# A graph-attention layer: ten sets of adjacency rows loaded with the projection, the first unit made by blocks, s and t read by ScalarE and compared by GpSimd, later q stores held back

## Chip, core and metric

The kernel runs on one core of a Trainium2 chip. The time is device microseconds of one launch. Its engines are TensorE (PE; PEld is its weight load), VectorE (DVE), ScalarE (ACT), GpSimd (POOL) and SyncE (SP), which only issues transfers. GpSimd issues transfers too.

## What is computed

The inputs are `x` (8192 x 256, float32), an adjacency matrix `adj` (8192 x 8192, int32) of zeros and ones, and the parameters of one attention layer.

```python
h = jnp.maximum(_layernorm(x, axis=-1), 0.0)
Wh = h @ W_w + W_b
e = leaky_relu((Wh @ a1)[:, None] + (Wh @ a2)[None, :], negative_slope=0.2)
attention = jnp.where(adj > 0, e, NEG)
attention = jax.nn.softmax(attention, axis=1)
out = x + attention @ Wh
```

## The kernel before

The work has two stages.

**The projection** goes over the 64 blocks of 128 rows of x, in 32 pairs p. VectorE makes the layer norm's statistics and factors (`norms`; nine groups, `GROUPS`, of 4, 4 and then 8 blocks; the last step of a group, L464, releases the blocks of it). GpSimd (`normalise`, L279; ScalarE for the first four blocks) applies the factors. TensorE transposes a pair (L747), ScalarE copies it out with the relu (`copy_hT`, L329), and TensorE multiplies it by the weights (`project`, L756). Two extra columns of the product are s and t, the two halves of e. VectorE reads them out of PSUM (`read_s_t`, L479), takes the smaller t of the pair (`greater_t`, L484; t is carried with its sign turned), ScalarE makes exponentials of it (`column_exps`, L334) and scales the product into the high half of a split float16 pair (`x_high`, L339), and VectorE makes the low half (`x_low`, L489), which frees the PSUM slot; there are six slots. In the course of it GpSimd issues the loads of the first eight sets of adjacency rows (a set is 128 rows by a quarter of the columns, 256 KB as read, issued as 4 quadrants by `load_quadrant`, L285), and VectorE transposes them (`transpose`, L586) beside the last eight pairs.

Between the stages, VectorE reduces t over all columns and makes q, a factor of each row. SyncE stores the first piece of q to memory, loads it back broadcast over the partitions (`load_q`, L229) and stores the rest. GpSimd's further loads wait for that load.

**The attention** has 8 rows s of 1024 output rows each, and in each row 32 units k of 2 blocks of 128 columns. A unit is made in a ring of four: ScalarE makes the products (`product`, L362, two halves of 1024), VectorE the weights (`weights`, L656), ScalarE their high half (`high`, L377), VectorE the low half (`low`, L663); then TensorE does 48 matmuls on it (`unit`, L789). Eight units are a chunk g; while a chunk is made, VectorE transposes the eight sets of the next (`turn`). TensorE sums all of a row into the eight PSUM banks. At the end of a row VectorE divides and adds x (`finish`, L671 and L674), and the next row's first matmul of a bank (`start`, L793) waits for that. After the projection VectorE also makes a mean (L643 to L647) which TensorE's first `start` needs.

The order on each engine is the order in which the code is written: no scheduler moves anything. Every engine works through its own list and waits on semaphores.

## Time and profile before

| | |
|---|---|
| median of 3 runs | 1485.84 us (1485.68 to 1487.18) |
| the profiled execution | 1486.66 us |
| its span, first to last instruction | 1484.9 us |
| TensorE busy | 98% |
| VectorE busy | 96% |
| ScalarE busy | 73% |
| GpSimd busy | 41% |
| mean granted TensorE clock | 0.992 of full speed |

A matmul counts as busy while it is modelled to run, so 98% says that TensorE nearly always has work, not that it runs at its peak. The busy shares are means over stages with different limits: the projection lasts to 91 us of the span, the first attention row to 283 us, and the seven other rows fill the rest.

### The profile page before, as it was taken

Reading aid. Unit: us, or ns where it says so; the run is one execution under the profiler, and the core shown is the slowest. Engines: PE = TensorE matmul, PEld = TensorE weight load, DVE = VectorE, ACT = ScalarE, POOL = GpSimd, SP = SyncE. Lnnn points to the kernel's source line nnn. Section 1 sums busy time; section 2 is a strip of 40 time slices with the busy share of each in tenths; the row PEclk is TensorE's granted clock in tenths of the full one; section 3 lists DMA queues with packets and bytes.
Section 4 is the critical chain, followed back from the end, with each engine's and each line's share of the span. In section 5 each row is a group of like instructions: output and inputs, shape, how many; then the busy total and the mean of one; then the engine's idle time right before and its main releaser. Section 6 shows DMA issues by size and latency. Waiting matters only on the chain.

```text
span 1484.9 us, 29899 instructions
## 1 busy us (share of the span) xinstructions
PE 1450.0 (98%) x12746; PEld 1261.6 (85%) x12746; DVE 1421.7 (96%) x1263; ACT 1086.0 (73%) x1006; POOL 605.4 (41%) x1106
## 2 busy tenths in 40 slices
PE   6969999999999999999999999999999999999998
PEld 5848888888888888888888888888888888888887
DVE  8989999999999999999999999999999999999993
ACT  4768888687777777687776877777776877777771
POOL 4748444354443444354442544344432544433000
PEclk9989999999999999999999999999999999999999
DMA  9729997798778977799777977699677887788000
GB/s 215 86 26 131 98 73 55 108 82 61 51 65 102 84 51 51 85 97 69 52 64 95 86 53 51 60 117 75 48 61 102 77 61 51 51 102 70 2 1 29
DMA packets 179559, 107.53 MB, mean 72 GB/s; under 512 B 20065, under 2 KB 176353, under 8 KB 179425
## 3 DMA queue, kind: packets, MB, share of 16 engines
q0 software_dynamic: 155904, 75.56, 68.1%
q1 hardware_dynamic: 23520, 30.05, 6.9%
q8 instruction: 100, 1.64, 0.4%
q14 instruction: 35, 0.28, 0.1%
HBM read 298.45 MB, written 8.42 MB: 207 GB/s over the span
## 4 chain that ended last, share of the span: by engine, by line
PE 81%; DVE 15%; DMA 1%; issue 1%; POOL 0%; SPq 0%; ACT 0%; DVEq 0%
PE acc L789 80%; DVE work L663 4%; DVE work L656 4%; DVE xr L437 1%; DVE adj_cols L586 1%; DVE X L489 1%; DMA adj_rows<-in_adj 1%; PE acc L756 1%; PE acc L793 0%; DVE xr L448 0%; DVE xr L484 0%; DMA work<-q_rows 0%; POOL adj_rows L285 0%; DVE xr L473 0%; DVE xr L469 0%
## 5 line engine op out<-in xcount | busy, mean ns | idle before, releaser
L789 PE MATMUL acc<-X,work 128*128 128x257 f16 x12288 | 1367.6, 273 | 7.1 <-DVE work L663 7.1
L789 PEld LDWEIGHTS acc<-X,work 128*128 128x128 f16 x12288 | 1189.8, 97 | 178.8 <-DVE work L663 7.6
L285 POOL DMA_DIRECT2D adj_rows<-in_adj x1024 | 551.3, 548 | 721.4 <-DVE adj_cols L586 684.8
L377 ACT ACTIVATE work<-work 128x2048 f16<-128x2048 f32 x256 | 488.0, 1909 | 292.2 <-PE acc L789 269.8
L663 DVE SCALAR_TENSOR_TENSOR work<-work 128x2048 f16<-128x2048 f32 x256 | 585.3, 2286 | 26.6 <-ACT work L377 26.5
L656 DVE SCALAR_TENSOR_TENSOR work<-work,sigma,adj_cols 128x2048 f32<-128x2048 f32 x256 | 595.1, 2325 | 5.7 <-ACT work L362 2.2
L362 ACT ACTIVATE work<-q_odd,r_j 128x1024 f32<-128x1024 f32 x256 | 278.5, 1135 | 23.9 <-DVE work L663 23.9
L362 ACT ACTIVATE work<-work,r_j 128x1024 f32<-128x1024 f32 x256 | 278.5, 1136 | 23.4 <-DVE work L663 18.2
L586 DVE STREAM_TRANSPOSE adj_cols<-adj_rows 128x512 int32<-128x512 int32 x256 | 177.1, 701 | 1.4 <-DMA adj_rows<-in_adj 1.4
L756 PE MATMUL acc<-q_odd,adj_cols 128*128 128x258 f32 x256 | 64.4, 396 | 0.7 <-ACT adj_cols L329 0.6
L756 PEld LDWEIGHTS acc<-q_odd,adj_cols 128*128 128x128 f32 x256 | 48.0, 197 | 8.7 <-ACT adj_cols L329 2.1
L279 POOL TENSOR_SCALAR work<-work,xr 128x256 f32<-128x256 f32 x60 | 33.6, 564 | 32.4 <-DVE xr L464 31.3
L747 PE MATMUL acc<-q_odd,work 128*128 128x128 f32 x128 | 21.5, 289 | 13.2 <-ACT work L320 9.9
L747 PEld LDWEIGHTS acc<-q_odd,work 128*128 128x128 f32 x128 | 16.2, 146 | 18.4 <-issue 11.9
L437 DVE BATCH_NORM_STATS2 xr<-work 128x6 f32<-128x256 f32 x64 | 25.4, 417 | 3.9 <-DMA work<-in_x 3.7
L489 DVE SCALAR_TENSOR_TENSOR X<-acc,c_j,X 128x256 f16<-128x256 f32 x64 | 28.6, 473 | 0.0
L334 ACT ACTIVATE c_j<-xr 128x2 f32<-128x2 f32 x32 | 9.5, 296 | 25.8 <-DVE xr L484 25.3
L674 DVE SCALAR_TENSOR_TENSOR xr<-acc,rden,xr 128x256 f32<-128x256 f32 x64 | 26.6, 478 | 0.6
L339 ACT ACTIVATE X<-acc,c_j 128x256 f16<-128x256 f32 x64 | 26.8, 476 | 0.0
L329 ACT ACTIVATE adj_cols<-acc 128x256 f32<-128x256 f32 x64 | 23.4, 369 | 0.1
L295 POOL DMA_DIRECT2D xr<-in_L_gnn_W_b x16 | 21.4, 1622 | 1.0 <-issue 1.0
L793 PE MATMUL acc<-mean_wh,tiny 128*128 128x257 f16 x64 | 17.2, 291 | 2.8 <-DVE mean_wh L647 1.6
(76 smaller groups left out, 84.4 us busy)
## 6 DMA issues: line engine op xcount, KB each, us to landing
adj_rows<-in_adj POOLq DMA_DIRECT2D x1024, 64.0 KB, 4.2
xr<-in_x SPq DMA_DIRECT2D x16, 512.0 KB, 4.6
xr<-in_L_gnn_W_b POOLq DMA_DIRECT2D x16, 512.0 KB, 17.0
out<-xr SPq DMA_DIRECT2D x16, 512.0 KB, 5.4
work<-in_x SPq DMA_DIRECT2D x28, 256.0 KB, 15.1
work<-q_rows SPq DMA_DIRECT2D x4, 512.0 KB, 5.4
q_odd<-q_rows SPq DMA_DIRECT2D x4, 512.0 KB, 5.7
work<-in_x SPq DMA_DIRECT2D x8, 128.0 KB, 3.3
```

The costliest lines, as they stand in the source:

```text
L279: nc.gpsimd.tensor_scalar(x_in[:, b, :], x_in[:, b, :], rstd[:, b:b + 1], shift[:, b:b + 1], ALU.mult, ALU.add).then_inc(s_hp, 1)
L285: pool.dma_start(rows8[QP * q:QP * (q + 1), n % R8], adj_v[s, m, k, q]).then_inc(s_rows[n % R8], 16)
L362: ins = nc.scalar.mul(Wt[:, i % RING, e, :], q_bc[s % 2], r_j[:, 2 * k + e:2 * k + e + 1])
L377: nc.scalar.mul(Et[:, at:at + 2, 0, :], Wt[:, i % RING], SCALE).then_inc(s_H, 1)
L437: nc.vector.bn_stats(st[:, b % XG + n, :], x_in[:, b + n, :]).then_inc(s_bn, 1)
L489: nc.vector.scalar_tensor_tensor(out=X16[:, b, 1, 0:F], in0=ps_wh[:, b % WH, 0:F], scalar=c_j[:, b:b + 1], in1=X16[:, b, 0, 0:F], op0=ALU. ...
L586: nc.vector.transpose(rows.rearrange("p w (q r) -> p q w r", q=SQ), rows8[:, n % R8].bitcast(I32).rearrange("p q (w c) -> p q w c", w=CW)) ...
L656: nc.vector.scalar_tensor_tensor(out=slot, in0=slot, scalar=sigma[:, k:k + 1], in1=edges, op0=ALU.max, op1=ALU.min).then_inc(s_M, 1)
L663: nc.vector.scalar_tensor_tensor(out=Et[:, at:at + 2, 1, :], in0=Wt[:, i % RING], scalar=SCALE, in1=Et[:, at:at + 2, 0, :], op0=ALU.mult, ...
L747: ins = nc.tensor.transpose(ps_hT[p % 2][:, (2 * c + e) * P:(2 * c + e + 1) * P], x_in[:, b, c * P:(c + 1) * P], ident)
L756: ins = nc.tensor.matmul(ps_wh[:, b % WH, 0:F2], hT[:, p % 2, c, e * P:(e + 1) * P], Wx[:, c, :], start=(c == 0), stop=(c == KF - 1))
L789: return nc.tensor.matmul(acc[:, m, 0:F1], Et[:, 2 * (k % RING) + e, 1 if n == 2 else 0, m * P:(m + 1) * P], X16[:, 2 * k + e, 1 if n == 1 ...
```

## The change

It has five parts.

1. `read_s_t` moves from VectorE to ScalarE, and `greater_t` from VectorE to GpSimd. On ScalarE, `copy_hT` of the pair after next now stands ahead of `column_exps`. GpSimd's `greater_t(p)` stands ahead of the normalisation of block 2p + 8.
2. Ten sets of adjacency rows instead of eight are loaded in the course of the projection: GpSimd issues a quadrant behind three of four blocks, instead of two of three. VectorE transposes the two added sets between the denominator columns and the mean.
3. The first unit of the first row is made in two blocks, with semaphores of their own, so that each step and TensorE's first 24 matmuls wait for one block only.
4. On ScalarE the product of unit 2 now stands behind both high halves of unit 0.
5. SyncE stores the rest of q only when the loaded q has landed.

```diff
+    AHEAD = 10
@@ SyncE
             load_q(0)
+            sp.wait_ge(s_q, 16)
             store_q(0, NZ // 2, NZ, s_qst)
@@ GpSimd
+            def greater_t(p):
+                pool.wait_ge(s_st, p + 1)
+                if p == 0:
+                    pool.wait_ge(s_lnx, 1)
+                nc.gpsimd.tensor_scalar(t_top[:, p:p + 1], s_t[:, 2 * p, 1:2], s_t[:, 2 * p + 1, 1:2], sc[:, 12:13],
+                                        ALU.min, ALU.add).then_inc(s_tt, 1)
             for b in range(4, NB):
+                if b >= 8 and b % 2 == 0:
+                    greater_t(b // 2 - 4)
                 normalise(b)
-                turn, at = divmod(b - 4, 3)
-                if at < 2 and 2 * turn + at < NQ * SETS:
-                    load_quadrant(*divmod(2 * turn + at, NQ))
+                turn, at = divmod(b - 4, 4)
+                if at < 3 and 3 * turn + at < NQ * AHEAD:
+                    load_quadrant(*divmod(3 * turn + at, NQ))
+            for p in range(PAIRS - 4, PAIRS):
+                greater_t(p)
             pool.wait_ge(s_q, 16)
-            for n in range(SETS, NSET * NS):
+            for n in range(AHEAD, NSET * NS):
@@ ScalarE
             for p in range(PAIRS + 1):
+                if p >= 1:
+                    read_s_t(p - 1)
                 if p >= 2:
                     x_high(2 * p - 4)
                     x_high(2 * p - 3)
+                if p + 1 < PAIRS:
+                    copy_hT(p + 1)
                 if p >= 1:
                     column_exps(p - 1)
-                if p + 1 < PAIRS:
-                    copy_hT(p + 1)
...
-            product(0, 0)
+            act.wait_ge(s_q, 16)
+            nc.scalar.mul(Wt[:, 0, 0, :], q_bc[0], r_j[:, 0:1]).then_inc(s_W0, 1)
+            nc.scalar.mul(Wt[:, 0, 1, :], q_bc[0], r_j[:, 1:2]).then_inc(s_W, 1)
+            act.wait_ge(s_M0, 1)
+            nc.scalar.mul(Et[:, 0, 0, :], Wt[:, 0, 0, :], SCALE).then_inc(s_H0, 1)
+            act.wait_ge(s_M, 1)
+            nc.scalar.mul(Et[:, 1, 0, :], Wt[:, 0, 1, :], SCALE).then_inc(s_H, 1)
             product(0, 1)
-            high(0, 0)
             product(0, 2)
             high(0, 1)
@@ VectorE
                 norms(p, 0)
-                if p >= 1:
-                    read_s_t(p - 1)
                 norms(p, 1)
-                if p >= 1:
-                    greater_t(p - 1)
                 norms(p, 2)
...
+            for m in range(AHEAD - SETS):
+                transpose(1, m)
             dve.wait_ge(s_tot, 1)
...
-                if g + 1 < NC * NS:
+                if g + 1 < NC * NS and SETS * g + m >= AHEAD - SETS:
                     transpose(g + 1, m)
...
-            weights(0, 0)
+            first_weights(0, s_W0, s_M0)
+            first_weights(1, s_W, s_M)
+            first_low(0, s_H0, s_E0)
+            first_low(1, s_H, s_E)
@@ TensorE
-            unit(0, 0)
+            pe.wait_ge(s_E0, 1)
+            block_of_unit(0, 0)
+            pe.wait_ge(s_E, 1)
+            block_of_unit(0, 1)
```

GpSimd's list in the middle of the projection. `work<-work,xr` is `normalise` of one block, `DMA` one quadrant of rows. Before:

```order
L279 TENSOR_SCALAR work<-work,xr 128x256 [waits norm_factors_ready] x2
L285 DMA adj_rows<-in_adj 32x4x512
L279 TENSOR_SCALAR work<-work,xr 128x256 [waits norm_factors_ready]
L285 DMA adj_rows<-in_adj 32x4x512
L279 TENSOR_SCALAR work<-work,xr 128x256 [waits norm_factors_ready] x2
```

Now (`xr<-xr,sc 128x1` is `greater_t`):

```order
L293 TENSOR_SCALAR xr<-xr,sc 128x1 [waits s_t_read]
L285 TENSOR_SCALAR work<-work,xr 128x256 [waits norm_factors_ready]
L299 DMA adj_rows<-in_adj 32x4x512
L285 TENSOR_SCALAR work<-work,xr 128x256 [waits norm_factors_ready]
L299 DMA adj_rows<-in_adj 32x4x512
L293 TENSOR_SCALAR xr<-xr,sc 128x1 [waits s_t_read]
L285 TENSOR_SCALAR work<-work,xr 128x256 [waits norm_factors_ready]
L299 DMA adj_rows<-in_adj 32x4x512
L285 TENSOR_SCALAR work<-work,xr 128x256 [waits norm_factors_ready]
```

A comparison now stands ahead of every second block and waits for ScalarE's read, and the quadrants stand closer.

VectorE's list from the end of the mean's preparation to unit 3's weights. `X<-c_j,X` is the last instruction ahead of the mean, the `mean_wh` rows are the mean, `work` rows are weights (with `sigma`) and low halves. Before:

```order
L641 TENSOR_TENSOR X<-c_j,X 128x64 [waits vector_chain]
L643 CAST mean_wh<-sc 1x1 [waits mean_wh_in_psum]
L647 TENSOR_TENSOR mean_wh<-mean_f,xr 1x256
L656 SCALAR_TENSOR_TENSOR work<-work,sigma,adj_cols 128x2048 [waits adj_transposed,products_ready] x2
L663 SCALAR_TENSOR_TENSOR work<-work 128x2x1024 [waits weights_hi_ready]
L586 STREAM_TRANSPOSE adj_cols<-adj_rows 128x4x4x32 [waits adj_loaded8]
L656 SCALAR_TENSOR_TENSOR work<-work,sigma,adj_cols 128x2048 [waits adj_transposed,products_ready]
L663 SCALAR_TENSOR_TENSOR work<-work 128x2x1024 [waits weights_hi_ready]
L586 STREAM_TRANSPOSE adj_cols<-adj_rows 128x4x4x32 [waits adj_loaded9]
L656 SCALAR_TENSOR_TENSOR work<-work,sigma,adj_cols 128x2048 [waits adj_transposed,products_ready]
L663 SCALAR_TENSOR_TENSOR work<-work 128x2x1024 [waits weights_hi_ready]
```

Now:

```order
L655 TENSOR_TENSOR X<-c_j,X 128x64 [waits vector_chain]
L602 STREAM_TRANSPOSE adj_cols<-adj_rows 128x4x4x32 [waits adj_loaded8]
L602 STREAM_TRANSPOSE adj_cols<-adj_rows 128x4x4x32 [waits adj_loaded9]
L659 CAST mean_wh<-sc 1x1 [waits mean_wh_in_psum]
L663 TENSOR_TENSOR mean_wh<-mean_f,xr 1x256
L744 SCALAR_TENSOR_TENSOR work<-work,sigma,adj_cols 128x1024 [waits adj_transposed,first_block_product_ready]
L744 SCALAR_TENSOR_TENSOR work<-work,sigma,adj_cols 128x1024 [waits adj_transposed,products_ready]
L749 SCALAR_TENSOR_TENSOR work<-work 128x1024 [waits first_block_hi_ready]
L749 SCALAR_TENSOR_TENSOR work<-work 128x1024 [waits weights_hi_ready]
L672 SCALAR_TENSOR_TENSOR work<-work,sigma,adj_cols 128x2048 [waits adj_transposed,products_ready] x2
L679 SCALAR_TENSOR_TENSOR work<-work 128x2x1024 [waits weights_hi_ready]
```

Two transposes moved ahead of the mean, and unit 0's low half stands ahead of unit 1's weights, both in halves.

ScalarE's list from the loaded q on; `128x2x1024` rows are high halves, the others products. Before:

```order
L362 ACTIVATE work<-work,r_j 128x1024 [waits q_loaded,r_and_sigma_ready]
L362 ACTIVATE work<-work,r_j 128x1024 x3
L377 ACTIVATE work<-work 128x2x1024 [waits weights_ready]
L362 ACTIVATE work<-work,r_j 128x1024 x2
L377 ACTIVATE work<-work 128x2x1024 [waits weights_ready]
```

Now:

```order
L421 ACTIVATE work<-work,r_j 128x1024 [waits q_loaded,r_and_sigma_ready]
L422 ACTIVATE work<-work,r_j 128x1024
L424 ACTIVATE work<-work 128x1024 [waits first_block_weights_ready]
L426 ACTIVATE work<-work 128x1024 [waits weights_ready]
L387 ACTIVATE work<-work,r_j 128x1024 x4
L402 ACTIVATE work<-work 128x2x1024 [waits weights_ready]
```

Unit 0's two high halves moved ahead of units 1 and 2's four products; behind the last row the list goes on as before, with the products of units 3 and 4 and then unit 2's high half.

## Rows read from the trace of the kernel before

**Rows 1.** Late in row 0: busy us of PE, PEld, DVE, ACT, POOL; clock, DMA share, GB/s.

```profile
240.00:280.00 40.00, 40.00 (x364) 34.97 (x363) 39.90 (x24) 30.21 (x24) 17.16 (x32) 1.00 0.76 66
```

**Rows 2.** Timeline, change from the first to the second attention row (start, duration).

```profile
267.83 14.54 PE L789 MATMUL acc<-X,work 128*128 128x257 f16 x130
...
282.94 1.66 DVE L674 SCALAR_TENSOR_TENSOR xr<-acc,rden,xr 128x256 f32<-128x256 f32 x4
...
283.57 0.27 PE L793 MATMUL acc<-mean_wh,tiny 128*128 128x257 f16 x1 [1.20 <-DVE xr L674]
```

**Rows 3.** Waits of TensorE from 120 us to the end (total, times, longest).

```profile
PE acc L793 <- DVE xr L674: 1.2, 1, 1.2
```

**Rows 4.** Timeline of TensorE, two of the last pairs of the projection.

```profile
83.41 1.91 PE L756 MATMUL acc<-q_odd,adj_cols 128*128 128x258 f32 x8
...
87.78 3.65 PE L756 MATMUL acc<-q_odd,adj_cols 128*128 128x258 f32 x16
```

**Rows 5.** Timeline of ScalarE, one round of the projection.

```profile
61.58 0.29 ACT L334 ACTIVATE c_j<-xr 128x2 f32<-128x2 f32 x1 [0.70 <-DVE xr L484]
...
62.49 0.84 ACT L339 ACTIVATE X<-acc,c_j 128x256 f16<-128x256 f32 x2
63.39 0.30 ACT L334 ACTIVATE c_j<-xr 128x2 f32<-128x2 f32 x1
```

**Rows 6.** Groups of VectorE by line, 0 to 90 us (busy us, mean ns).

```profile
L484 DVE TENSOR_SCALAR xr<-xr,sc 128x1 f32<-128x1 f32 x31 | 8.1, 260 | 0.2
...
L479 DVE COPY xr<-acc 128x4 f32<-128x4 f32 x31 | 4.4, 141 | 1.0 <-PE acc L756 0.9
```

**Rows 7.** Timeline of GpSimd, first blocks of two groups of the layer norm.

```profile
33.07 0.56 POOL L279 TENSOR_SCALAR work<-work,xr 128x256 f32<-128x256 f32 x1 [3.42 <-DVE xr L464]
33.56 0.56 POOL L285 DMA_DIRECT2D adj_rows<-in_adj  x1
34.16 0.55 POOL L279 TENSOR_SCALAR work<-work,xr 128x256 f32<-128x256 f32 x1
...
79.81 4.31 POOL L279 TENSOR_SCALAR work<-work,xr 128x256 f32<-128x256 f32 x8 [3.52 <-DVE xr L464]
```

**Rows 8.** Groups of GpSimd by line, 0 to 90 us, the smallest instructions.

```profile
L273 POOL TENSOR_SCALAR_AFFINE_SELECT q_odd<-q_odd 128x128 f32<-128x128 f32 x1 | 0.3, 288 | 0.2 <-POOL q_odd L271 0.2
...
L845 POOL MEMSET const-float32-1.0<- 128x1 f32 x1 | 0.1, 98 | 0.0
```

**Rows 9.** Timeline, from the last pair to the load of q.

```profile
90.89 0.70 DVE L586 STREAM_TRANSPOSE adj_cols<-adj_rows 128x512 int32<-128x512 int32 x1
...
91.68 0.22 DVE L603 TENSOR_REDUCE ext<-xr 128x1 f32<-128x64 f32 x1
...
97.47 0.34 SPq L229 DMA_DIRECT2D work<-q_rows  x1
```

**Rows 10.** Stretches of 1 us while q is loaded (columns as rows 1).

```profile
99.00:100.00 1.00, 0.94 (x3) 0.22 (x1) 0.02 (x1) 0.00 (x0) 0.00 (x0) 0.50 0.81 307
100.00:101.00 1.00, 0.00 (x0) 0.00 (x0) 0.93 (x4) 0.00 (x0) 0.00 (x0) 0.50 1.07 172
```

**Rows 11.** Timeline, from the loaded q to unit 2's low half.

```profile
101.10 0.41 DVE L647 TENSOR_TENSOR mean_wh<-mean_f,xr 1x256 f16<-1x256 f32 x1
101.51 4.26 ACT L362 ACTIVATE work<-work,r_j 128x1024 f32<-128x1024 f32 x4 [5.14 <-DMA work<-q_rows]
...
103.73 4.61 DVE L656 SCALAR_TENSOR_TENSOR work<-work,sigma,adj_cols 128x2048 f32<-128x2048 f32 x2 [2.21 <-ACT work L362]
...
110.61 39.56 PE L789 MATMUL acc<-X,work 128*128 128x257 f16 x341 [7.13 <-DVE work L663]
...
115.97 1.89 ACT L377 ACTIVATE work<-work 128x2048 f16<-128x2048 f32 x1
117.14 0.71 DVE L586 STREAM_TRANSPOSE adj_cols<-adj_rows 128x512 int32<-128x512 int32 x1 [0.61 <-DMA adj_rows<-in_adj]
...
120.00 2.28 DVE L663 SCALAR_TENSOR_TENSOR work<-work 128x2048 f16<-128x2048 f32 x1
```

More of the change, by code:

```diff
@@ L685, in chunk @@
                     weights(g, i + 1)
-                    low(g, i)
+                    if g + i:
+                        low(g, i)
                     turn(g, i)
@@ L721, in chunk_after_last, with first_weights, first_low @@
                 low(g, 7)
-            weights(0, 0)
+            def first_weights(e, made, done):
+                dve.wait_ge(made, 1)
+                dve.wait_ge(s_T, SETS)
+                nc.vector.scalar_tensor_tensor(out=Wt[:, 0, e, :], in0=Wt[:, 0, e, :], scalar=sigma[:, 0:1],
+                                               in1=cols8[:, 0, 0, :, e], op0=ALU.max, op1=ALU.min).then_inc(done, 1)
+            def first_low(e, made, done):
+                dve.wait_ge(made, 1)
+                nc.vector.scalar_tensor_tensor(out=Et[:, e, 1, :], in0=Wt[:, 0, e, :], scalar=SCALE, in1=Et[:, e, 0, :],
+                                               op0=ALU.mult, op1=ALU.subtract).then_inc(done, 1)
+            first_weights(0, s_W0, s_M0)
+            first_weights(1, s_W, s_M)
+            first_low(0, s_H0, s_E0)
+            first_low(1, s_H, s_E)
             for g in range(NC * NS):
@@ L805, in first_units, with block_of_unit @@
                 ins.then_inc(s_pe, 1)
+            def block_of_unit(k, e):
+                for m in range(M):
+                    for n in range(3):
+                        ins = part(m, k, e, n)
+                return ins
             def unit(s, k):
                 pe.wait_ge(s_E, NK * s + (k + 1))
-                for e in range(2):
-                    for m in range(M):
-                        for n in range(3):
-                            ins = part(m, k, e, n)
-                return ins
+                block_of_unit(k, 0)
+                return block_of_unit(k, 1)
             def last_units(s):
```

18 lines of the change are left out of this document (8 added, 10 removed).

## Prediction, made before the changed kernel was run

> **What bounds the kernel now.** I read the chain that ended last first, in order of time. From 283.84 us on it is TensorE alone, 170.8 us a row. Before that it is VectorE. The stretch late in row 0 shows why: VectorE is busy 39.90 of 40 us, and TensorE 40.00 [rows 1]. So both look like the bound. The timeline at the change of rows decides: TensorE ends row 0 at 267.83 + 14.54 = 282.37, VectorE's division (in its list behind everything that it makes for row 0) comes only at 282.94, and TensorE starts row 1 at 283.57, after 1.20 idle [rows 2]. That is the only wait of TensorE from 120 us to the end [rows 3]. So the end lies where VectorE's list of row 0 ends, plus seven full rows of TensorE. VectorE has not waited since about 118 us; what starts its list sooner there moves the end, and what only starts TensorE sooner does not.
>
> Ahead of that stand three stages in series: the projection (VectorE's reduction of t at 91.68 [rows 9]), the way of q through memory (loaded, 101.51) and the first units, which VectorE makes to 120.00, the start of unit 2's low half [rows 11]; from there its list is the same in both kernels.
>
> **Projection.** At its end TensorE sets the pace: two pairs from 83.41 to 87.78, 2.18 us a pair, and it ends at 87.78 + 3.65 = 91.43 [rows 4]. In the middle it does not. GpSimd gets the factors of a group of four pairs at 33.07 and of the fifth group after it at 79.81 [rows 7]: 46.74 / 20 = 2.34 us a pair, 9.35 a group. VectorE is that pace, with ScalarE waiting for `greater_t` (0.70 in the round shown [rows 5]).
>
> VectorE loses two small instructions a pair, 141 and 260 ns long [rows 6]. They overlap their neighbours, so I count 0.24 us a pair of the list. That alone is 2.10 a pair, under TensorE's 2.18. The new pace must then be looked for on the other engines.
>
> - ScalarE: a round is 63.39 - 61.58 = 1.81 with little waiting inside [rows 5]; the new read of four elements takes a place of about 0.15 to 0.3 (L334's row with two elements is 0.29 long). I take 1.95 to 2.0.
> - GpSimd: a normalisation holds its list 0.50 and a quadrant 0.60 [rows 7]. A group now has 8 x 0.50 + 6 x 0.60 = 7.6 (5.3 quadrants before), and four comparisons. The trace has none on GpSimd: a fill of one element takes 0.10, 256 elements of the same kind of operation 0.56 [rows 7, 8]. It is nearest to the short end, as it has one element: 0.15 to 0.2 with its wait. With that, 8.2 to 8.4 a group, under TensorE's 8.73.
> - The loop through all of them. GpSimd's comparison of a group's second pair stands behind two normalisations that need the group's factors, where it used to wait for no factors. From ScalarE's start of a round: read 0.2, two high parts 0.85; VectorE's second low part starts at 1.3, the factors are there 1.0 later (a low part and three dependent small steps, estimate) at 2.3; GpSimd then has 0.5 + 0.6 + 0.5 + 0.6 + the comparison 0.2 = 4.7; ScalarE's exponentials end at 5.0. The two rounds left of the group take 3.9 to 4.0. That is 9.0 a group, 0.35 less than now, and a bit more than TensorE's 8.73.
>
> VectorE gains 1.1 ahead of the first of the six factor releases (4.5 pairs x 0.24), then 5 x 0.35 = 1.75. The last release comes 2.8 sooner, at 77.0. Behind it ScalarE still catches up, and I take 2.4 for TensorE's end: 89.0. Something is given back there. The high parts of pair 29 used to need only the exponentials; now they stand behind the read of pair 30, so VectorE's low parts end just past 89.05 and the last transpose (0.70 [rows 9]) is done at 89.75. The reduction starts 0.75 behind TensorE's end, against 91.68 - 91.43 = 0.25. So 91.68 becomes 89.75: **1.9 us**. Ends: if the handshakes eat what VectorE gains, -0.5 (the end part alone); if TensorE becomes the pace all the way and the end is no later, 2.7.
>
> **Load of q.** From 97.47 to 101.51 it takes 4.04 us [rows 9, 11]. The stretch at 99 moves 307 GB/s, the next 172 at a DMA share of 1.07: the small pieces of the four other stores are between [rows 10]. Had the second stretch gone on at 307 it would have carried its bytes in 0.56 us. I take **0.7** with a bit of the tail. Ends: 0, and 1.2. Further it can't help: VectorE's mean ends at 101.51 [rows 11] and the first weights, 1.26 behind the load, would then wait for it. The two transposes put ahead of the mean (1.24) lie in VectorE's wait for TensorE's mean product (1.47) and cost nothing; if that cover were gone they would cost at most this 1.24. The held stores land later, and with them q of row 1 and SyncE's x rows; both are wanted over 100 us later.
>
> **First units**, counted from the loaded q. Before: VectorE starts unit 2's low half at 120.00 - 101.43 = 18.57. On that way it waited 2.21 at first, transposed two sets, and waited for both (0.61 at the second) [rows 11]. Now, with a product 1.04 (4.26 for four), a high half 1.9, weights 2.25 (4.61 for two), and half of each for a block: products at 1.2 and 2.3; block weights to 2.5 and 3.65; high halves to 3.55 and 4.7; low halves to 4.8 and 5.95. ScalarE goes on with four products to 8.8, VectorE makes units 1's weights from 6.8 to 9.1, ScalarE unit 1's high half to 11.05, VectorE unit 1's low half from 11.35 to 13.6 and unit 3's weights to 15.85. ScalarE has four more products ahead of unit 2's high half (11.05 + 4.15 = 15.2, done 17.15), so VectorE waits 1.3 and starts unit 2's low half at 17.2: **1.4 us** sooner, not the 2.7 that its own work allows (15.85). Ends: 1.0 and 1.8. TensorE starts at 4.9 behind the load instead of 110.61 - 101.43 = 9.2. It then has to wait for unit 1 at about 12 and for unit 2 at 19; that costs nothing, since it has the 1.20 of rows 2 to spare and gains about 2 here. A clock that falls in such a pause is also inside this. The third set of rows is now the first that GpSimd asks for behind q, and is wanted 19 us later; before, two sets took 15.6 us [rows 11].
>
> **Sum.** 1.9 + 0.7 + 1.4 = 4.0 us of the profiled execution's 1486.66, whose span is 1484.9: span 1480.9. That execution lies 0.8 above the median of 1485.84, so the median becomes 1481.8.
>
> **Rivals.**
> - A: the projection keeps its pace. For it: the loop's 9.0 is an addition of eight steps, and 0.35 more makes it 9.35. Against it: VectorE's list is shorter in any case. Then 0.7 + 1.4 and -0.5: 1.6 us, 1484.2.
> - B: GpSimd becomes the pace. From the first factor release of rows 7 (33.07 - 1.1 = 32.0) to the second block of the last group it has 42 normalisations, 31 quadrants and 20 comparisons: 32.0 + 21.0 + 18.6 + 20c = 71.6 + 20c. Now that point is 79.81 + 1.0 = 80.8. With c = 0.56, the long end, it is 82.8; the last pairs are 2.0 later, the end part another 0.5, and 2.1 is won behind: 0.4 slower, 1486.2. At c = 0.7 it is 85.6 and the kernel 3.2 us slower; from there the change loses by what can be measured, and a wait that GpSimd pays at each of 32 semaphores would do it. The rows speak for a small c, as above.
> - C: more is won: TensorE paces the projection and the load is as short as its bytes: 2.7 + 1.2 + 1.5 = 5.4, 1480.4.
>
> With VectorE's 0.26 doubled for GpSimd, c would be 0.52. The Trainium skill says in "GPSIMD Engine Reference", Engine selection, that elementwise work belongs on VectorE and GpSimd is about twice slower; by that rule rival B's sum comes out near 1485.4, no change. No row here shows a one-element operation on both engines.
>
> **Chances.** Forecast 0.52, A 0.24, B 0.14 (half of it slower by more than 3 us), C 0.10. What a measurement of this kernel can tell from no change is about 0.2%, 3.0 us, so the line is at 1482.9. The forecast's own range is 1480.6 to 1483.3, a small part of it beyond the line. Faster: 0.63; within 0.2%: 0.28; slower: 0.09. The range from 1479.9 to 1484.9 holds the forecast, C and most of A.
>
> **What the profile would show.** GpSimd's first block of the last group (79.81) near 77.0; the comparison on GpSimd under 0.25 us; VectorE's reduction near 89.8; load of q near 3.3 us; unit 2's low half 17.2 behind the load, with a wait for ScalarE ahead of it; TensorE's first wait at the row change longer than 1.20, and still for VectorE's division. Wrong would be: GpSimd without idle time in the projection (B), ScalarE waiting for GpSimd over 1 us a pair (A), or a row-0 end set by TensorE, with which only TensorE's own start counts.

## The result, and the profile after

The changed kernel takes 1488.33 us (median of 22 runs, 1487.63 to 1488.90), the kernel before 1486.17 (22 runs, 1485.33 to 1487.78). The ratio is 1.0014, 95% interval 1.0008 to 1.0021: 2.2 us slower, clear of the noise, inside the prediction's line of 0.2%, and outside the predicted range on the side of slower. The forecast was 4.0 us faster.

The profiled execution of the changed kernel took 1487.63 us with a span of 1485.8, so the traces differ by only 0.9 us of span. Before's traced execution lies 0.5 above its median and after's 0.7 below; what the traces can explain is 1.0 of the 2.2 us, and the other 1.2 are where these two executions lie among the runs. Why the usual executions differ by more than these two is open. In a second series, at the end of the experiments, the change was 1.3 us slower, which by itself is not clear of the noise.

Timeline from the last pair to the first units, of the changed kernel (start, duration, engine, line, operation, and in brackets the idle time before it and who ended it):

```profile
90.00 3.65 PE L788 MATMUL acc<-q_odd,adj_cols 128*128 128x258 f32 x16
...
93.94 0.18 DVE L618 TENSOR_REDUCE ext<-xr 128x1 f32<-128x64 f32 x1
...
98.15 0.31 SPq L243 DMA_DIRECT2D q_rows<-q_j  x1
...
100.42 0.34 SPq L234 DMA_DIRECT2D work<-q_rows  x1
...
103.84 1.15 ACT L421 ACTIVATE work<-work,r_j 128x1024 f32<-128x1024 f32 x1 [5.26 <-DMA work<-q_rows]
...
108.71 6.99 PE L821 MATMUL acc<-X,work 128*128 128x257 f16 x48 [3.02 <-DVE work L749]
...
117.58 4.60 PE L821 MATMUL acc<-X,work 128*128 128x257 f16 x40 [1.88 <-DVE work L679]
...
120.99 2.29 DVE L679 SCALAR_TENSOR_TENSOR work<-work 128x2048 f16<-128x2048 f32 x1 [1.21 <-ACT work L402]
```

Against [rows 4, 9, 11]: TensorE ends the projection 2.22 later (93.65 for 91.43), the reduction comes 2.26 later (93.94 for 91.68), the loaded q 2.33 later (103.84 for 101.51), unit 2's low half 0.99 later (120.99 for 120.00). So more than two microseconds are lost before the reduction, and 1.34 are won back behind the loaded q.

The change of rows, and the only wait of TensorE from 125 us to the end (total, times, longest), against [rows 2, 3]:

```profile
283.92 1.66 DVE L690 SCALAR_TENSOR_TENSOR xr<-acc,rden,xr 128x256 f32<-128x256 f32 x4
284.55 0.27 PE L825 MATMUL acc<-mean_wh,tiny 128*128 128x257 f16 x1 [1.73 <-DVE xr L690]
```

```profile
PE acc L825 <- DVE xr L690: 1.7, 1, 1.7
```

TensorE's first matmul of row 1 moved from 283.57 to 284.55, by 0.98: the 0.99 of unit 2's low half, carried through VectorE's full list. That part of the reading holds. The question is the projection.

Its middle, on GpSimd of the changed kernel. A group is four pairs, eight blocks; VectorE releases it with the last step of its factors. Between the two rows that waited for VectorE's factors (51.47 and 61.08) lies one group:

```profile
51.47 0.56 POOL L285 TENSOR_SCALAR work<-work,xr 128x256 f32<-128x256 f32 x1 [0.34 <-DVE xr L495]
51.97 0.57 POOL L299 DMA_DIRECT2D adj_rows<-in_adj  x1
52.59 0.55 POOL L285 TENSOR_SCALAR work<-work,xr 128x256 f32<-128x256 f32 x1
53.09 0.58 POOL L299 DMA_DIRECT2D adj_rows<-in_adj  x1
53.71 0.37 POOL L293 TENSOR_SCALAR xr<-xr,sc 128x1 f32<-128x1 f32 x1
54.06 0.55 POOL L285 TENSOR_SCALAR work<-work,xr 128x256 f32<-128x256 f32 x1
...
58.30 0.38 POOL L293 TENSOR_SCALAR xr<-xr,sc 128x1 f32<-128x1 f32 x1
58.67 0.55 POOL L285 TENSOR_SCALAR work<-work,xr 128x256 f32<-128x256 f32 x1
...
61.08 0.56 POOL L285 TENSOR_SCALAR work<-work,xr 128x256 f32<-128x256 f32 x1 [0.35 <-DVE xr L495]
```

A group takes 61.08 - 51.47 = 9.61 us, where it took 9.35 [rows 7] and 9.0 was predicted. The comparison (L293, one element per partition) is 0.37 long and holds the list for 0.35: 53.71 to 54.06. I had put 0.15 to 0.2. GpSimd sits idle for 0.35 of the 9.61, so its own list is 9.26 long (8.2 to 8.4 in the prediction). Who waits, in ScalarE's timeline of the same stretch and in the waits of 0 to 90 us:

```profile
54.11 0.30 ACT L357 ACTIVATE c_j<-xr 128x2 f32<-128x2 f32 x1 [1.06 <-POOL xr L293]
...
56.11 0.29 ACT L357 ACTIVATE c_j<-xr 128x2 f32<-128x2 f32 x1
...
58.71 0.30 ACT L357 ACTIVATE c_j<-xr 128x2 f32<-128x2 f32 x1 [0.70 <-POOL xr L293]
58.91 0.14 ACT L353 COPY xr<-acc 128x4 f32<-128x4 f32 x1
```

```profile
POOL work L285 <- DVE xr L495: 19.6, 8, 13.7
ACT c_j L357 <- POOL xr L293: 16.9, 18, 3.4
...
DVE X L509 <- ACT X L362: 8.4, 8, 1.5
```

ScalarE's exponentials wait for the group's first comparison (1.06) and again for its third (0.70). VectorE, in the same stretch:

```profile
54.95 0.88 DVE L509 SCALAR_TENSOR_TENSOR X<-acc,c_j,X 128x256 f16<-128x256 f32 x2 [1.22 <-ACT X L362]
...
59.55 0.48 DVE L509 SCALAR_TENSOR_TENSOR X<-acc,c_j,X 128x256 f16<-128x256 f32 x1
...
60.85 0.13 DVE L495 SCALAR_TENSOR_TENSOR xr<-xr 128x8 f32<-128x8 f32 x1
```

So the pace is set by a loop: factors released, GpSimd, ScalarE, VectorE, next factors released. It is longer than the one I drew, and two ways through it are nearly equal in length.

- Through three comparisons. GpSimd does six normalisations, five quadrants and *three* comparisons (51.47 to 58.68), ScalarE makes exponentials and high parts, VectorE two low parts and the last steps of the next factors (61.08). That is 7.21 on GpSimd and 2.40 on the others. As a formula with c for one comparison: 9.61 = 8.5 + 3 x 0.37.
- Through one comparison and VectorE's own list. From the release to the exponentials behind the first comparison 2.64 (51.47 to 54.11), to VectorE's low part 0.84 (54.95), and from there VectorE's list to the next release, 6.04, in which the profile shows no wait, and 0.09 to GpSimd's block.

VectorE waits once a group, for the high part behind the first comparison. The low part at 59.55 follows its high part as closely as the one at 54.95 does (0.51), so it is held by the third comparison too, but by no more than 0.07: VectorE's instruction ahead of it started 0.40 earlier, and one round before, where it waits for nothing, the same two stand 0.33 apart. Without its second and third comparison the loop would thus still be 9.5 long, an estimate from this trace.

### The profile page after: what moved, and what is told of

The parts are those of the page before. It is cut to its first block, busy times and chain, and to the rows that moved or that the text cites. A ratio compares the mean times of both kernels' runs of the same rounds, so it can differ in the third digit from the quotient of the medians.

```text
span 1485.8 us, 29904 instructions
## 1 busy us (share of the span) xinstructions
PE 1451.5 (98%) x12746; PEld 1260.3 (85%) x12746; DVE 1414.9 (95%) x1201; ACT 1089.8 (73%) x1039; POOL 616.9 (42%) x1138
## 4 chain that ended last, share of the span: by engine, by line
PE 81%; DVE 14%; issue 1%; ACT 1%; POOL 1%; DMA 1%; SPq 0%; DVEq 0%; ACTq 0%
PE acc L821 80%; DVE work L672 4%; DVE work L679 4%; DVE adj_cols L602 2%; DVE X L509 1%; DVE xr L468 1%; DMA work<-in_x 0%; PE acc L788 0%; POOL work L285 0%; PE acc L825 0%; ACT work L387 0%; POOL adj_rows L299 0%; SPq L222 0%; ACT work L402 0%; DVE xr L479 0%
## 5 line engine op out<-in xcount | busy, mean ns | idle before, releaser
L825 PE MATMUL acc<-mean_wh,tiny 128*128 128x257 f16 x64 | 17.2, 291 | 3.4 <-DVE xr L690 1.7
```

## The experiments

The theory after the first reading (G in the expectations) is that GpSimd paces the projection through its comparisons, by the way through three of them. The rivals are that ScalarE's new order and its read do (S), that the added quadrants do (Q), and that the way of q or the first units lost the time. H is the theory that holding the stores shortens the load of q. Each kernel has its own runs of the kernel before beside it; the first four share 1486.40, the next four 1487.33, the last four 1486.78. The diffs show the lines that carry each edit; the definitions that move with them are left out.

**Comparison back on VectorE, all else as changed.**

```diff
@@ GpSimd
-                if b >= 8 and b % 2 == 0:
-                    greater_t(b // 2 - 4)
@@ VectorE
                 norms(p, 1)
+                if p >= 1:
+                    greater_t(p - 1)
                 norms(p, 2)
```

> The changed kernel with the comparison put back on VectorE, in its old place behind the statistics; the read of s and t stays on ScalarE. Theory G: the pace of the projection is a loop through GpSimd's list, release of a group's factors, six normalisations, five quadrants and three comparisons of 0.36 us, ScalarE, VectorE's low parts, next release; 9.61 us a group. Without the comparisons in it the loop is gone, TensorE (8.73) or VectorE (near 8.9) sets the pace: 9.0 a group or less, last pair about 3.5 us sooner than with the change, median 1484.5 to 1485.3. Rival Q: the denser quadrants alone make GpSimd late; then 9.4 a group or more, 1487.5. Rival S: the read and the order on ScalarE cost it; then no change, 1488.3.

1485.40 us against 1486.40, ratio 0.9992 (0.9983 to 1.0001). GpSimd's first blocks of two groups:

```profile
50.88 0.55 POOL L285 TENSOR_SCALAR work<-work,xr 128x256 f32<-128x256 f32 x1 [1.00 <-DVE xr L483]
...
59.70 0.55 POOL L285 TENSOR_SCALAR work<-work,xr 128x256 f32<-128x256 f32 x1 [1.00 <-DVE xr L483]
```

8.82 a group instead of 9.61, with 1.00 idle on GpSimd, and the reduction at 91.19 instead of 93.94. The read of s and t on ScalarE and the ten sets are still in it. This one part moved the reduction by 2.75 us. The median is 1.0 below the kernel before, which these runs just can't tell from nothing; against the change it is 3.2 better, each taken against the runs of before beside it. TensorE takes 8.82 for four pairs as well (50.65 to 59.47), where it had 8.73 at its own pace [rows 4]:

```profile
50.65 1.91 PE L785 MATMUL acc<-q_odd,adj_cols 128*128 128x258 f32 x8
...
59.47 1.91 PE L785 MATMUL acc<-q_odd,adj_cols 128*128 128x258 f32 x8
```

Neither TensorE's matmuls nor VectorE wait for anything here: both lists are full, and the profile's own chain runs through VectorE from 48 to 62 us. Which of the two sets the 8.82 is not shown.

**The comparison made twice on GpSimd** (the first result is read by nobody, so the outputs are unchanged).

```diff
+                nc.gpsimd.tensor_scalar(sc[:, 30:31], s_t[:, 2 * p, 1:2], s_t[:, 2 * p + 1, 1:2], sc[:, 12:13],
+                                        ALU.min, ALU.add)
                 nc.gpsimd.tensor_scalar(t_top[:, p:p + 1], ...
```

> The changed kernel with every comparison on GpSimd issued twice, the first into a cell that nobody reads. Theory G: three more of 0.36 us in the loop, 10.7 us a group, five groups and the pairs around them, about 6 us slower: 1494 to 1495. Rival: if GpSimd's list has room (Q and S false too, TensorE sets the pace), under 1 us slower, 1489.

1494.84 us, ratio 1.0057 (1.0044 to 1.007): 6.5 us over the change for 32 more comparisons, 0.20 each. The last factors come at 87.88 instead of 81.46, the reduction at 100.64 instead of 93.94. A group, from one first comparison to that of the next group, now takes 10.79:

```profile
51.44 0.37 POOL L293 TENSOR_SCALAR sc<-xr,sc 128x1 f32<-128x1 f32 x1
51.80 0.39 POOL L295 TENSOR_SCALAR xr<-xr,sc 128x1 f32<-128x1 f32 x1
...
62.23 0.37 POOL L293 TENSOR_SCALAR sc<-xr,sc 128x1 f32<-128x1 f32 x1
```

That is 1.18 more than 9.61. The way through three comparisons, with three more, gives 1.1 more (10.7), GpSimd's whole list with four more 1.44 on top of 9.26 (10.7); the way through one comparison and VectorE's list would give 9.9 and drops out. The first two say the same. The waits from 0 to 90 us show which holds:

```profile
ACT c_j L359 <- POOL xr L295: 23.5, 25, 3.3
POOL work L285 <- DVE xr L497: 16.6, 3, 13.9
```

GpSimd waited for factors 3 times instead of 8: here rival B of the prediction, GpSimd as the bound, has come true, and ScalarE waits for it 25 times. So this run does not show that three comparisons lie on the loop of the change; it shows what happens when GpSimd's list is full.

**Eight sets, all else as changed.**

```diff
-    AHEAD = 10
+    AHEAD = 8
-                turn, at = divmod(b - 4, 4)
-                if at < 3 and 3 * turn + at < NQ * AHEAD:
-                    load_quadrant(*divmod(3 * turn + at, NQ))
+                turn, at = divmod(b - 4, 3)
+                if at < 2 and 2 * turn + at < NQ * AHEAD:
+                    load_quadrant(*divmod(2 * turn + at, NQ))
```

> The changed kernel with eight sets instead of ten loaded with the projection, so a quadrant behind two of three blocks as before, and no transposes ahead of the mean. Theory G: the loop holds four or five quadrants of 0.61 instead of five, 9.1 to 9.4 us a group, last pair 1.5 to 2 us sooner; the first chunk takes back its two transposes and their wait, which ScalarE's lateness hides in part: 0.5 to 1.4 us. Sum 0.3 to 1.5 faster than the change, about 1487.5. Rival Q: the quadrants are the whole cause: a group at 9.0 or less, about 1486.5. If the sets were free: 1489 or more.

1486.99 us, ratio 1.0002 (0.9993 to 1.0011). The quadrants are in the loop too: with fewer of them a group takes 9.40 at the same place (50.90 to 60.30), and the reduction comes at 92.26. That is still later than before's 91.68. So beside the comparison the added quadrants cost a part. It is not so without it: with the comparison on VectorE a group takes less time with ten sets than with eight, 8.82 in the first experiment for 9.33 (a mean of four) in the eight-set variant below.

**The start by blocks alone:** parts 1, 2 and 5 of the change undone, parts 3 and 4 kept.

```diff
-    AHEAD = 10
+    AHEAD = 8
@@ SyncE
             load_q(0)
-            sp.wait_ge(s_q, 16)
@@ GpSimd
-                if b >= 8 and b % 2 == 0:
-                    greater_t(b // 2 - 4)
@@ ScalarE, with its order as before
-                if p >= 1:
-                    read_s_t(p - 1)
@@ VectorE
                 norms(p, 0)
+                if p >= 1:
+                    read_s_t(p - 1)
                 norms(p, 1)
+                if p >= 1:
+                    greater_t(p - 1)
```

> The kernel before with parts 3 and 4 alone: the first unit by blocks and ScalarE's order. From the loaded q, unit 2's low half starts at 17.2 us with the two added sets; here VectorE also has to transpose these two sets (1.3) and may wait for their rows: it started at 18.57 before. My expectation is 18 to 19 and a change within 0.5 us of the kernel before, 1486.2; the rival is that the blocks alone carry the 1.3 us, 1484.9.

1486.51 us, ratio 0.9999 (0.9991 to 1.0008): nothing gained. The trace, of an execution 1.2 above this median, says why:

```profile
106.36 7.81 PE L818 MATMUL acc<-X,work 128*128 128x257 f16 x48 [2.87 <-DVE work L746]
...
112.60 0.71 DVE L597 STREAM_TRANSPOSE adj_cols<-adj_rows 128x512 int32<-128x512 int32 x1 [1.89 <-DMA adj_rows<-in_adj]
...
117.81 5.92 PE L818 MATMUL acc<-X,work 128*128 128x257 f16 x37 [3.63 <-DVE work L676]
118.22 0.71 DVE L597 STREAM_TRANSPOSE adj_cols<-adj_rows 128x512 int32<-128x512 int32 x1 [0.47 <-DMA adj_rows<-in_adj]
...
121.08 2.28 DVE L676 SCALAR_TENSOR_TENSOR work<-work 128x2048 f16<-128x2048 f32 x1
```

By 112.60 - 1.89 = 110.71 VectorE has made unit 0 and unit 1's weights, where it had done the same at 110.55 before (111.39 - 0.84): the blocks start TensorE sooner, not VectorE's next unit. Then it waits for the ninth set's rows, 1.89 here and 0.84 before, in transfers that no run here takes apart, and 0.47 for the tenth's. Unit 2's low half stands 19.59 behind the first product (121.08 - 101.49), where it was 18.49 before [rows 11]. Where the two sets are there already, in the change and in the first experiment, it stands 17.15 behind. So in the traces the start by blocks needs the ninth and tenth set to be there; the medians of these runs are too close to show it.

**The stores of q not held back, all else as changed.**

```diff
             load_q(0)
-            sp.wait_ge(s_q, 16)
```

> The changed kernel without part 5: the other q stores are issued right behind the load of q. With the change the load takes 3.4 us, before 4.0; but with eight sets and the stores held it took 3.9. Theory H (holding the stores shortens the load): back to about 4.0, first units 0.6 later, median 0.5 slower than the change, 1488.8. Rival (the load is short for another reason that goes with the ten sets): load still 3.4 to 3.5, no change, 1488.3.

1488.55 us, ratio 1.0009 (1.0 to 1.0018), against 1.0014 (1.0008 to 1.0021) and, in a second series below, 1.0008 for the change itself: no difference that these runs can tell. In the trace the load takes 4.24 us (100.85 to 105.09) where it takes 3.42 held, and 3.41 to 3.73 in all nine traces with ten sets and held stores. So holding the stores is worth 0.5 to 0.8 with ten sets, close to the 0.7 predicted. With eight it is worth nothing that shows: 3.90 and 4.07 held in the two kernels with eight sets, 4.04 [rows 9, 11] and 4.00 not held. In the traces the gain does reach the end of row 0: TensorE starts row 1 at 285.81 here, 1.26 and 1.09 behind the two traces of the change. That the medians don't show it is open.

**The comparison a pair earlier on GpSimd**, ahead of block 2p + 6 instead of 2p + 8. It opens the loop: a group's second comparison now stands ahead of the first block that needs the group's factors.

```diff
-                if b >= 8 and b % 2 == 0:
-                    greater_t(b // 2 - 4)
+                if b >= 6 and b % 2 == 0:
+                    greater_t(b // 2 - 3)
```

> The changed kernel with GpSimd's comparison of a pair one pair earlier in its list. The loop from release to release then holds two comparisons and fewer blocks, about 7.0 us, and can't be the pace. If only the loop costs, a group falls to 8.8 and the median to 1485. If GpSimd's own list is the bound next, its 8 normalisations, 6 quadrants and 4 comparisons are 9.26 us busy in a group of 9.61, so a group comes to about 9.3, last pair 1.5 to 2 us sooner, median 1486.5. If neither, 1488.3.

1486.94 us, ratio 0.9999 (0.9991 to 1.0008). GpSimd from one group to the next, one comparison each:

```profile
50.50 0.37 POOL L293 TENSOR_SCALAR xr<-xr,sc 128x1 f32<-128x1 f32 x1
50.84 0.56 POOL L285 TENSOR_SCALAR work<-work,xr 128x256 f32<-128x256 f32 x1
...
59.84 0.37 POOL L293 TENSOR_SCALAR xr<-xr,sc 128x1 f32<-128x1 f32 x1
60.19 0.56 POOL L285 TENSOR_SCALAR work<-work,xr 128x256 f32<-128x256 f32 x1
```

9.34 a group, and no wait of GpSimd in it: its own list is the pace. The reduction is 1.25 earlier than in the change (92.69). So the loop did cost, 0.27 a group; and with it open, GpSimd still has 9.3 us of work in a group that TensorE does in 8.8.

**All but the moves:** read and comparison on VectorE as before, everything else as changed.

```diff
-                if b >= 8 and b % 2 == 0:
-                    greater_t(b // 2 - 4)
@@ ScalarE, with its order as before
-                if p >= 1:
-                    read_s_t(p - 1)
@@ VectorE
                 norms(p, 0)
+                if p >= 1:
+                    read_s_t(p - 1)
                 norms(p, 1)
+                if p >= 1:
+                    greater_t(p - 1)
```

> The changed kernel with part 1 undone: s and t read and compared on VectorE as before, all else as changed. Theory G: the projection is back at 9.35 us a group and ends 2 us sooner than with the change, the first units start as with it: median near 1486, level with the kernel before or 0.5 faster. Rival Q (the denser quadrants slow the projection by themselves): 1487.5 or more.

1486.75 us, ratio 0.9995 (0.9986 to 1.0004). 9.11 a group, and the reduction at 92.39. The first experiment differs from it in the read on ScalarE and ScalarE's order only, and has the reduction 1.20 sooner. So ScalarE's order and read are not the cause of the loss: together they gain 1.2 us in the traces. In the medians, each against the runs of before beside it, the first experiment is 1.0 faster and this one 0.6, so that the gain is likely there and not shown in time. The move of the comparison lost more.

**ScalarE's high half of unit 2 ahead of two more products**, on top of the first experiment. It aims at the wait of 1.21 that VectorE has ahead of unit 2's low half.

```diff
             product(0, 3)
+            high(0, 2)
             product(0, 4)
+            product(0, 5)
...
-                    if g == 0 and i == 0:
+                    if g == 0 and i <= 1:
                         continue
```

> The changed kernel with the comparison on VectorE (1485.4), and on ScalarE unit 2's high half ahead of unit 4's products instead of behind them. VectorE's wait of 1.21 us ahead of unit 2's low half should go, as the high half is ready 2.1 us sooner; its list of row 0 then ends 1.2 sooner, and TensorE, which had 1.75 to spare at the change of rows, follows: 1484.2. If TensorE's clock falls in its pause between units 0 and 1 (it did with eight sets), TensorE sets the end of row 0 and less comes out, 1485.0.

1484.24 us, ratio 0.9979 (0.997 to 0.9988).

```profile
101.54 1.15 ACT L409 ACTIVATE work<-work,r_j 128x1024 f32<-128x1024 f32 x1 [5.95 <-DMA work<-q_rows]
...
114.69 1.89 ACT L390 ACTIVATE work<-work 128x2048 f16<-128x2048 f32 x1
...
117.41 2.28 DVE L678 SCALAR_TENSOR_TENSOR work<-work 128x2048 f16<-128x2048 f32 x1
```

The low half starts 15.87 behind the first product and waits for nobody; in the change and in the first experiment it was 17.15. TensorE starts row 1 at 281.07, 1.16 before the first experiment's 282.23; the median is 3.1 below the runs of before beside it, the first experiment's 1.0 below its own.

**Three variants of that kernel, and the change once more, on one chip.** A quadrant behind every block, so that the loads are all asked for by block 43:

```diff
-                turn, at = divmod(b - 4, 4)
-                if at < 3 and 3 * turn + at < NQ * AHEAD:
-                    load_quadrant(*divmod(3 * turn + at, NQ))
+                if b - 4 < NQ * AHEAD:
+                    load_quadrant(*divmod(b - 4, NQ))
```

> The kernel with the comparison on VectorE and the high half ahead (1484.2), with a quadrant behind every block: the ten sets are asked for by block 43 instead of 57. It asks why the first q store takes 2.3 to 2.8 us to land in every kernel with ten sets and 1.5 to 1.6 in every one with eight. If it is the time since the last load of rows (16 us with ten, 20 and more with eight): the store lands in 1.6, the load of q takes 3.9. If it is the number of loads: 2.3 or more. GpSimd then has 8.9 us of list in a group while they last, 0.1 over the pace: 0.3 slower at most. Median 1483.5 to 1484.7.

1484.24 us, ratio 0.9981 (0.9972 to 0.999). The same time, and the load that waits for the first store of q is still issued 2.48 us behind that store.

Eight sets in it instead of ten:

```diff
-    AHEAD = 10
+    AHEAD = 8      (and a quadrant behind two of three blocks)
```

> The kernel with the comparison on VectorE and the high half ahead (1484.2), with eight sets instead of ten. The store should land in 1.6 us and the load take 3.9, 0.5 together sooner; VectorE has two more transposes and a wait for rows (1.5 to 1.9 at the first) in its first chunk, and TensorE a pause of 3 us between units 0 and 1 in which its clock falls. Slower by 1 to 2 us, 1485.2 to 1486.2. If ten sets were worth nothing: 1484.2 or less.

1485.39 us, ratio 0.999 (0.9982 to 0.9999). The added sets are worth 1.15 us once the comparison is off GpSimd (1484.24 with a quadrant behind every block, on the same chip). VectorE waits 0.84 for the ninth set's rows, and TensorE pauses 3.53:

```profile
111.54 0.71 DVE L600 STREAM_TRANSPOSE adj_cols<-adj_rows 128x512 int32<-128x512 int32 x1 [0.84 <-DMA adj_rows<-in_adj]
...
116.75 7.02 PE L820 MATMUL acc<-X,work 128*128 128x257 f16 x50 [3.53 <-DVE work L678]
```

In the traces the difference lies behind the loaded q: it is loaded at 101.48 here and at 101.39 there, and unit 2's low half follows after 17.98 here and 15.87 there. The middle of the projection is slower too (9.33 a group). One small step of VectorE's factors, a `tensor_scalar` of 128x8, takes 0.60 to 0.88 in the four middle groups here and at most 0.33 in the same kernel with ten sets (0.17 in the change). VectorE's list grows by it. What lengthens it is not taken apart by any run.

TensorE waiting for all of unit 0 instead of its first block:

```diff
-            pe.wait_ge(s_E0, 1)
-            block_of_unit(0, 0)
-            pe.wait_ge(s_E, 1)
-            block_of_unit(0, 1)
+            unit(0, 0)
```

> The kernel with the comparison on VectorE and the high half ahead (1484.2), with TensorE's first 24 matmuls waiting for the whole unit 0, as before the change; the other engines keep the blocks. TensorE starts 1.1 us later and its pause ahead of unit 1 is shorter. VectorE's list is the same and sets the end of row 0, so: no change, within 0.3. If the early start of TensorE carried the gain: 1 us slower, 1485.3. If the clock falls in the pause in many runs: a bit faster, 1483.8, with a smaller spread.

1484.03 us, ratio 0.998 (0.9971 to 0.9989), runs from 1483.69 to 1484.48. It costs nothing to start TensorE 1.0 later (107.42 for 106.42 in the kernel with the high half ahead): the pause ahead of unit 1 goes, and TensorE idles 1.01 at the change of rows here and 1.00 there. This is the lowest median, level with the two kernels at 1484.24 within the noise, 2.75 us below the kernel before and 4.1 below the change beside it. It beats both by leaving the comparison on VectorE and taking ScalarE's high half of unit 2 forward; the rest is the change.

The change itself again, for a second trace:

> The changed kernel as it is, once more, for a second trace. In the first one TensorE's clock held in its pauses between units 0, 1 and 2, and that execution lay 0.7 under the kernel's median. If the clock falls there in a typical run, this trace shows 0.50 in a stretch between 112 and 124 us and the end of row 0 set by TensorE; if not, the same as the first: 1.7 us idle at the change of rows. Median 1488.3.

1488.10 us, ratio 1.0008 (0.9999 to 1.0017). The projection and the end agree with the first trace within 0.2 us: releases at 32.09, 41.71, 51.32 and 60.94, reduction at 93.79, and

```profile
284.72 0.27 PE L825 MATMUL acc<-mean_wh,tiny 128*128 128x257 f16 x1 [1.75 <-DVE xr L690]
```

TensorE's first unit does not agree: its 48 matmuls take 8.33 us for 6.99, because the granted clock stays at 0.50 until 114 us instead of 111, and the pause ahead of unit 1 shrinks from 1.88 to 0.53. It costs nothing: row 1 starts 163.6 behind unit 2's low half in both traces. A fall of the clock behind the pause, which would cost time, was seen in neither trace.

## Why the prediction was wrong, by its own steps

Of the three terms of the sum, the projection's 1.9 us became 2.3 lost, the 0.7 of the load of q became 0.1 lost, and the 1.4 of the first units came as 1.3.

**Where the end lies** was right for the change. Its only wait of TensorE after 125 us is the one for VectorE's division, and that moves with unit 2's low half: 120.99 and 284.55 in the change, 117.41 and 281.07 in the faster kernel (3.58 and 3.48). One kernel is outside it: with eight sets and all else changed TensorE does not wait there at all, so its own start and clock set the end. With the doubled comparison and with the stores not held it still waits, 0.5.

**The group's 9.0 us** is the step that failed: 9.61. The term in it that was wrong is "the two rounds left of the group take 3.9 to 4.0". They took 4.60: from 54.11 to 56.11, 2.00, as predicted, and from 56.11 to 58.71, 2.60. The other part of the sum, from one round's start over VectorE and GpSimd to the next group's exponentials, was put at 5.0 and took 5.01 (2.37 from 58.71 to 61.08, and 2.64 from 51.47 to 54.11). That this part fits is luck: the comparison in it was put 0.15 to 0.2 too short, and VectorE's part too long by about as much.

Three things were wrong behind this. The first is the size of the comparison on GpSimd, "0.15 to 0.2 with its wait". I bounded it by a fill (0.10) and an operation of 256 elements (0.56) [rows 7, 8] and took the short end because it has one element. It holds the list 0.35 to 0.37. The same instruction took 0.26 on VectorE [rows 6], so 1.4 times. The prediction had the Trainium skill's rule in "GPSIMD Engine Reference", Engine selection, as GpSimd about twice slower in elementwise work, with c = 0.52. That section says it of operations with two inputs and calls those with one input about level; it does not say which of the two a `tensor_scalar` is that reads its operands per partition. The measurement lies between: 0.15 to 0.2 above my value, and 0.15 below that one.

The second is that ScalarE does not run free in the two rounds. It waits 0.70 for the third comparison, which stands behind six normalisations and five quadrants. The third is VectorE's own list. I took it as relieved and left it out of the loop, but from the low part behind the first comparison to the release it needs 6.0. With c = 0.2 and the rest as in the trace, the way through three comparisons would give 9.1 and the way through VectorE's list 9.4 (estimates). So the price of the comparison alone does not explain the miss: had it been right, the middle groups would still have been no faster than before. No run has a cheaper comparison on GpSimd, so this is worked out and not tested; tested is that the loss goes with the comparison's place on GpSimd.

Release by release: the first came at 32.25, 0.82 sooner than before (1.1 predicted). The four groups behind it took 9.61 each; before they took 9.28 on average, as the 9.35 of the prediction has a longer fifth one in it (70.20 to 79.81, 9.61). That fifth one now takes 10.77 (70.69 to 81.46). So the last release came at 81.46, 1.65 later than before (predicted 77.0), and the fifth group alone has 1.16 of it. In the other traces the fifth group takes 9.55 to 9.61 with eight sets and the comparison on VectorE, 10.16 or 10.17 with ten sets (9.70 where they were asked for by block 43), 10.47 with eight sets and the comparison on GpSimd, and with both 10.77: the added sets and the comparison each have a part in it. I had it as a group like the others.

**The end of the projection:** I said that the reduction would come 0.75 behind TensorE's end. It came 0.29 behind (93.65, 93.94), as before. With TensorE's end at 93.65 instead of 89.0, the term "1.9 us won" became 2.26 lost. Experiment one is its test: with the comparison back on VectorE the reduction is at 91.19, 0.5 ahead of before.

**VectorE's relief** was right in kind. With only the read moved a group takes 8.82, near TensorE's 8.73. ScalarE's read of four elements took 0.14, just under the estimate of 0.15 to 0.3.

**Load of q:** 3.42 us for the predicted 3.3 (103.84 - 100.42), and with ten sets the stores' part in it is shown. In two stretches of the change and one of the kernel without the hold (PE, PEld, DVE, ACT, POOL, clock, DMA share, GB/s; [rows 10] are the same of before):

```profile
102.00:103.00 1.00, 0.15 (x1) 0.00 (x0) 0.77 (x3) 0.00 (x0) 0.00 (x0) 0.50 0.82 307
103.00:104.00 1.00, 0.21 (x2) 0.15 (x3) 0.69 (x3) 0.16 (x1) 0.00 (x0) 0.50 0.07 25
```

```profile
103.00:104.00 1.00, 0.00 (x0) 0.00 (x0) 0.91 (x3) 0.00 (x0) 0.00 (x0) 0.50 1.00 196
```

What I left out is the store ahead of it. From its issue to the issue of the load took 1.53 us (95.94 to 97.47) and now 2.27 (98.15 to 100.42). Together, store and load take 5.69 us for 5.57 before: the term of 0.7 became -0.1 (-0.4 in the second trace, with 2.48 and 3.52). The longer store goes with the ten sets. In all ten traces with ten sets it is 2.27 to 2.78, in the four with eight 1.50 to 1.57, held or not, with the loads asked for early or late. Loads and transposes of the two sets come and go together in these runs, so even which of them does it stays open.

**First units:** 17.15 behind the loaded q with a wait of 1.21 for ScalarE, predicted 17.2 with a wait of 1.3. This term, 1.4, held (1.34 of trace against trace, from the start of ScalarE's first product), and moving one high half showed the rest that the prediction had named (another 1.28). That it needs the added sets I had as a remark, not as a condition; with eight sets the start by blocks alone was worth nothing.

**TensorE's pauses** cost nothing in the change, as said: 1.88 before unit 1 (0.53 in the second trace), and the granted clock stays at 1.00 behind it. In the eight-set kernels the pause was longer. Windows of the change and of the start by blocks alone, behind the pause:

```profile
118.00:120.00 2.00, 2.00 (x20) 1.75 (x19) 1.78 (x1) 2.00 (x3) 2.00 (x5) 1.00 1.13 220
```

```profile
118.00:120.00 2.00, 2.00 (x12) 1.41 (x11) 1.78 (x2) 2.00 (x3) 2.00 (x5) 0.51 1.17 191
```

Behind 3.63 us of idle time TensorE made 12 matmuls in 2 us instead of 20, at a granted clock of 0.51, the level of 1.2 GHz. Its spare at the change of rows fell to 0.40 there, to 0.18 in the improved kernel with eight sets, and to nothing in the change with eight sets. So the cover that I named for the pauses is real, and used up or nearly so in those kernels.

**The sum of the traces:** +2.26 to the reduction, -0.05 from there to the store's issue, +0.74 for the store, -0.62 for the load, -1.34 from the first product to unit 2's low half: +0.99, which is the 0.98 at the change of rows and the 0.9 of span. Rival B's mechanism was closest, but its sum (GpSimd's list alone, 71.6 + 20 x 0.36 = 78.8) is 4.3 short of the 83.1 at which the trace ends the last group's second block. GpSimd was nearly full (9.26 of 9.61 a group), but what held was the loop.

## What to carry to other kernels

Taking work off the busiest engine helps only if the result does not come back through a queue that stands behind work of the next round. Write the loop down release by release, put the list of *every* engine on it between the same two points, and price the moved instruction by the nearest one of its kind on that engine, not by its element count. Here the read moved to ScalarE, with its order, was worth 1.2 us in the trace, and the comparison moved to GpSimd cost 2.75. Parts of a change can need each other: an earlier start was worth nothing until the rows for it were there, and those were worth 1.15 with it.

## What was not expected of the hardware

- A `tensor_scalar` of one element per partition takes 0.36 us on GpSimd and holds its list 0.35; 256 elements take 0.56 and hold it 0.50. So between these two sizes most of the price does not depend on the size. On VectorE the same instruction shows 0.26.
- The first store of q, issued behind the reduction, was 1.50 to 1.57 us on its way (to the issue of the load that waits for it) in the four traces with eight sets loaded and 2.27 to 2.78 in the ten with ten sets. The cause is open: asking for the sets earlier did not change it (2.48), and the change's own two traces have 2.27 and 2.48.
- A load of q that is held apart from four small stores took 0.5 to 0.8 us less with ten sets (3.41 to 3.73 for 4.24) and nothing less with eight (3.90 and 4.07 for 4.00 and 4.04). This is not explained either.
- TensorE's granted clock stayed at 1.00 behind the pause of 1.88 us in the change, and was 0.50 about a microsecond after one of 2.00 in the kernel without the hold. Both stand behind the 48 matmuls of unit 0.
- A `tensor_scalar` of 128x8 on VectorE, the same instruction with the same operands, took 0.17 in the middle groups of the change (and the step behind it 0.42), 0.48 to 0.52 in the kernel before and 0.60 to 0.88 in the improved kernel with eight sets. The kernels differ in what GpSimd does beside it; the cause is open.
